# Two-stage layer kernel: the first queries and four key tiles of the attention are fetched and split inside the projection

## What is computed

```
xn  = layernorm(x)
q, k, v = split(xn @ Wqkv + bqkv)            # each 4096 x 512
att = softmax(q @ k.T / sqrt(512)) @ v       # per sequence
z   = xn @ A_w.T                             # 64 experts x rank 8 = 512
z   = z * gate(xn)                           # top 16 of 64 experts, softmax weights
out = x + att @ Wo + bo + 2 * (z @ B_w.T)
```

## Time and profile before

| what | value |
|---|---|
| median of three runs | 2958.62 us |
| the profiled execution, its own time | 2959.48 us |
| its span, first to last instruction | 2957.6 us |
| mean granted TensorE clock | 0.983 |
| TensorE matmul busy | 2772.5 us (94%) |
| VectorE busy | 1858.8 us (63%) |
| ScalarE busy | 931.8 us (32%) |
| GpSimd busy | 736.4 us (25%) |
| DMA, mean over the span | 161 GB/s |

### The profile page before, as it was taken

The page is one execution under the profiler, slowest core; times in us unless marked ns, Lnnn a source line. Parts: engine busy times, 40 slices in busy tenths (PEclk is TensorE's granted clock), DMA queues, the critical chain, the costliest instruction groups (busy, mean ns, idle before and its releaser), DMA issues.

```text
span 2957.6 us, 34124 instructions
## 1 busy us (share of the span) xinstructions
PE 2772.5 (94%) x12096; PEld 2249.8 (76%) x12096; DVE 1858.8 (63%) x2133; ACT 931.8 (32%) x1164; POOL 736.4 (25%) x429
## 2 busy tenths in 40 slices
PE   2888999999999999999889999999999999999999
PEld 1666787878778787888668788787887878878787
DVE  5876777666776777364466655666556665566653
ACT  1222232323232223322244333343433434334331
POOL 7165212030120203020030502305033050330521
PEclk8999999999999999999999999999999999999999
DMA  9767455544554454333533534535445353453544
GB/s 371 232 234 237 153 192 166 183 138 152 187 180 142 163 177 137 115 99 107 180 105 121 174 131 137 178 121 174 130 136 177 122 176 128 136 176 124 175 143 136
DMA packets 261611, 476.34 MB, mean 161 GB/s; under 512 B 26864, under 2 KB 76016, under 8 KB 257264
## 3 DMA queue, kind: packets, MB, share of 16 engines
q1 hardware_dynamic: 223408, 372.45, 39.0%
q10 hardware_dynamic: 29376, 68.72, 6.6%
q0 software_dynamic: 8704, 33.56, 3.2%
HBM read 390.74 MB, written 83.91 MB: 160 GB/s over the span
## 4 chain that ended last, share of the span: by engine, by line
PE 74%; DVE 11%; DMA 4%; issue 4%; ACT 3%; SPq 2%; POOL 2%; DVEq 0%; ACTq 0%; POOLq 0%
PE psum L689 31%; PE psum L1448 13%; PE psum L1450 13%; PE psum L1449 13%; DVE prob L1645 3%; DVE w_lo L739 2%; PE psum L626 2%; DVE r_lo L1617 1%; ACT r_hi L1338 1%; SPq L362 1%; DVE s_lo L744 1%; DVE part L726 1%; DMA t_scratch<-xb 1%; DMA w_raw<-t_scratch 1%; DMA xb<-W_blocks 1%
## 5 line engine op out<-in xcount | busy, mean ns | idle before, releaser
L739 DVE TENSOR_TENSOR w_lo<-w_raw,w_hi 128x1024 fp32r<-128x1024 f32 x224 | 325.7, 1454 | 417.0 <-ACT w_hi L442 416.6
L442 ACT ACTIVATE w_hi<-w_raw 128x1024 fp32r<-128x1024 f32 x224 | 237.4, 1060 | 946.4 <-PE psum L689 812.7
L1617 DVE TENSOR_TENSOR r_lo<-r_raw,r_hi 128x1024 fp32r<-128x1024 f32 x256 | 380.3, 1500 | 189.4 <-ACT r_hi L1338 189.4
L1448 PE MATMUL psum<-r_hi,f_hi 128*128 128x512 f32 x1024 | 405.7, 396 | 30.4 <-DVE r_lo L1617 29.0
L1449 PE MATMUL psum<-r_lo,f_hi 128*128 128x512 f32 x1024 | 400.8, 391 | 0.0
L1450 PE MATMUL psum<-r_hi,f_lo 128*128 128x512 f32 x1024 | 400.6, 391 | 0.0
L689 PE MATMUL psum<-s_hi,w_hi 128*128 128x512 f32 x896 | 356.3, 398 | 40.8 <-DVE w_lo L739 27.6
L1583 POOL TENSOR_TENSOR res<-res,b_out 128x512 f32<-128x512 f32 x128 | 222.8, 1769 | 661.4 <-DMA res<-x 661.4
L689 PE MATMUL psum<-w_hi,s_hi 128*128 128x512 f32 x896 | 353.8, 395 | 32.5 <-DVE w_lo L739 32.4
L689 PE MATMUL psum<-s_lo,w_hi 128*128 128x512 f32 x896 | 352.9, 394 | 0.0
L689 PE MATMUL psum<-s_hi,w_lo 128*128 128x512 f32 x896 | 352.5, 393 | 0.0
(11 more groups left out here) (133 smaller groups left out, 4287.0 us busy)
## 6 DMA issues: line engine op xcount, KB each, us to landing
w_raw<-t_scratch SPq DMA_DIRECT2D x128, 512.0 KB, 3.9
w_raw<-W_blocks SPq DMA_DIRECT2D x96, 512.0 KB, 3.9
r_raw<-k_scratch SPq DMA_DIRECT2D x64, 512.0 KB, 3.8
r_raw<-v_scratch SPq DMA_DIRECT2D x64, 512.0 KB, 4.6
r_raw<-B_T SPq DMA_DIRECT2D x64, 512.0 KB, 3.9
res<-x SPq DMA_DIRECT2D x128, 256.0 KB, 4.9
r_raw<-Wo SPq DMA_DIRECT2D x64, 512.0 KB, 4.5
out<-res SPq DMA_DIRECT2D x128, 256.0 KB, 3.4
```

The source lines that it names most:

```text
L442: nc.scalar.activation(w_hi[:, s % RAW], w_raw[:, s % RAW], ACT.Copy).then_inc(s_whi, 1)
L739: nc.vector.tensor_tensor(w_lo[:, s % RAW], w_raw[:, s % RAW], w_hi[:, s % RAW].bitcast(F32), ALU.subtract).then_inc(s_wlo, 1)
L1448: pe.matmul(bank, sh, mh, start=first, stop=False)
L1617: nc.vector.tensor_tensor(r_lo[:, slot, :], r_raw[:, slot, :], r_hi[:, slot, :].bitcast(F32), ALU.subtract).then_inc(b_lo, 1)
```

## The change

SyncE, at step (5, 1) of the last group (the sixth of seven products), issues the fetch of the first queries and of key items 0 to 3, after waits for what must be free or stored. ScalarE and VectorE, in the steps of the last product, split them: at s = 1 and 2 the two halves of the queries, at s = 4 to 7 the four key items. The corresponding instructions at the start of phase B fall away. The tiles of phase B are declared in another order, so that each early tile lies over a block that is free by then: `r_lo` over `xb` 0, `q_raw` and `q_hi` over block 1, `r_raw` over block 2, `r_hi` over block 3, `q_lo` over `mean_rstd`. `early_stored` waits for the key and query stores of the groups before the last.

```diff
@@ phase_a, sync @@
                             store_kq(g, C22, b)
                             store_kq(g, C12, b)
+                    if not more and (idx, s) == (5, 1):
+                        ahead.sync(sp)
@@ phase_a, scalar (behind split_weights, split_x) @@
+                    if not more and idx == NI - 1:
+                        ahead.scalar(act, s)
@@ phase_a, vector (behind split_weights, take_last_side) @@
+                    if not more and idx == NI - 1:
+                        ahead.vector(dve, s)
@@ phase_a @@
     def early_stored(engine):
-        for c in (C11, C21):
-            engine.wait_ge(s_stK[c], 16 * HT * NG)
-        for c in (C22, C12):
+        for c in range(4):
             engine.wait_ge(s_stK[c], 16 * HT * (NG - 1))
...
+    first.queries_free = lambda engine: engine.wait_ge(s_slo, pair(NG - 1, 2, PART - 1) + 1)
+    first.queries_low_free = lambda engine: engine.wait_ge(s_xn[3], NG * PART)
+    first.raw_free = lambda engine: (engine.wait_ge(s_slo, pair(NG - 1, 3, PART - 1) + 1),
+                                     engine.wait_ge(s_s2, NG * PART))
+    first.high_free = lambda engine: (engine.wait_ge(s_slo, pair(NG - 1, 5, PART - 1) + 1),
+                                      engine.wait_ge(s_s1, NG * PART))
@@ phase_b @@
-    r_raw = sb("r_raw", [P, RING, 2 * W])
+    r_lo = sb("r_lo", [P, RING, 2 * W], F32R)
     q_raw = sb("q_raw", [P, DT, QG])
     q_hi = sb("q_hi", [P, DT, QG], F32R)
+    r_raw = sb("r_raw", [P, RING, 2 * W])
+    r_hi = sb("r_hi", [P, RING, 2 * W], F32R)
     q_lo = sb("q_lo", [P, DT, QG], F32R)
-    r_hi = sb("r_hi", [P, RING, 2 * W], F32R)
-    r_lo = sb("r_lo", [P, RING, 2 * W], F32R)
@@ phase_b, sync @@
-                fetch(t, i, k_scr.rearrange("(m p) t -> p m t", p=P)[:, :, bass.ds(base + i * 2 * P, 2 * P)])
+                if not (static(t) and t == 0 and i < RING):
+                    fetch_keys(t, i, base)
...
-        first.x_used(sp)
-        first.early_stored(sp)
-        queries(0)
+        if early:
+            first.early_stored(sp)
+            first.queries_free(sp)
+            queries(0)
+            first.raw_free(sp)
+            for i in range(RING):
+                fetch_keys(0, i, 0)
+            return
@@ phase_b, scalar @@
-        first.x_used(act)
-        split_queries(0, 0)
-        split_queries(0, 1)
+        if step is not None:
+            if step == 0:
+                first.queries_free(act)
+            if step in (1, 2):
+                split_queries(0, step - 1)
+            if step == 3:
+                first.high_free(act)
+            if step >= IPI - RING:
+                split(0, step - IPI + RING)
+            return
@@ phase_b, vector: the same, with queries_low_free at step 0 and x_used at step 3 @@
@@ phase_b, scores of scalar and vector @@
-            split(t, 0)
+            start = static(t) and t == 0
+            if not start:
+                split(t, 0)
             for i in range(S_IT):
-                if i + 1 < S_IT:
+                if i + 1 < S_IT and not (start and i + 1 < RING):
                     split(t, i + 1)
```

More of the change, by code:

```diff
@@ L93, in layer_kernel @@
         }
+        ahead = Programs()
         with ExitStack() as a_memory:
             first = phase_a(nc, a_memory, whole, psum, common, x, xT, W_blocks, b_cols, WqT, keysT,
-                            k_scr, q_scr, z_scr, v_scr, stat_scr, t_scr, T, C, D, NE, RD, RANK, KT, TG, NG)
-        second = phase_b(nc, whole, psum, common, first, x, Wo, bo, B_T, k_scr, q_scr, z_scr, v_scr, out,
+                            k_scr, q_scr, z_scr, v_scr, stat_scr, t_scr, ahead, T, C, D, NE, RD, RANK, KT, TG, NG)
+        second = phase_b(nc, whole, psum, common, first, ahead, x, Wo, bo, B_T, k_scr, q_scr, z_scr, v_scr, out,
                          T, C, D, S, QG, NQ, KEYT, DT)
@@ L145, in phase_a @@
 def phase_a(nc, memory, whole, psum, common, x, xT, W_blocks, b_cols, WqT, keysT,
-            k_scr, q_scr, z_scr, v_scr, stat_scr, t_scr, T, C, D, NE, RD, RANK, KT, TG, NG):
+            k_scr, q_scr, z_scr, v_scr, stat_scr, t_scr, ahead, T, C, D, NE, RD, RANK, KT, TG, NG):
     NTOK = TG // P
@@ L1117, in phase_a, with phase_b @@
     return first
-def phase_b(nc, whole, psum, common, first, x, Wo, bo, B_T, k_scr, q_scr, z_scr, v_scr, out,
+def phase_b(nc, whole, psum, common, first, ahead, x, Wo, bo, B_T, k_scr, q_scr, z_scr, v_scr, out,
             T, C, D, S, QG, NQ, KEYT, DT):
@@ L1139, in phase_b @@
     EXP_STEP = 4
+    IPI = 8
     def sb(name, shape, dt=F32):
@@ L1250, in out_ready, with sync @@
             engine.wait_ge(b_used, number(u + 1, S_IT + c * OPB + OPB - 1) + 1)
-    def sync(sp):
+    def sync(sp, early=False):
         def fetch(t, it, source):
@@ L1280, in load_block, with fetch_keys @@
                              ).then_inc(b_x[slot], 16)
+        def fetch_keys(t, i, base):
+            fetch(t, i, k_scr.rearrange("(m p) t -> p m t", p=P)[:, :, bass.ds(base + i * 2 * P, 2 * P)])
         def scores(t):
@@ L1331, in sync, with scalar @@
             sp.wait_ge(b_st[slot], 16 * NQ * CB * QT // XO)
-    def scalar(act):
+    def scalar(act, step=None):
         def split(t, it):
@@ L1376, in scores @@
         def scores(t):
-            split(t, 0)
+            start = static(t) and t == 0
+            if not start:
+                split(t, 0)
             for i in range(S_IT):
-                if i + 1 < S_IT:
+                if i + 1 < S_IT and not (start and i + 1 < RING):
                     split(t, i + 1)
-                if i == 0 and not (static(t) and t == 0):
+                if i == 0 and not start:
                     finish_values(t - 1)
@@ L1611, in gpsimd, with vector @@
         output(NQ - 1, False)
-    def vector(dve):
+    def vector(dve, step=None):
         def split(t, it):
@@ L1691, in scores @@
         def scores(t):
-            split(t, 0)
+            start = static(t) and t == 0
+            if not start:
+                split(t, 0)
             for i in range(S_IT):
-                if i + 1 < S_IT:
+                if i + 1 < S_IT and not (start and i + 1 < RING):
                     split(t, i + 1)
-                if i == 0 and static(t) and t == 0:
+                if i == 0 and start:
                     first.take_last(dve)
@@ L1747, in values @@
                     split_queries(t + 1, i - 5)
-        split_queries(0, 0)
-        split_queries(0, 1)
+        if step is not None:
+            if step == 0:
+                first.queries_low_free(dve)
+            if step in (1, 2):
+                split_queries(0, step - 1)
+            if step == 3:
+                first.x_used(dve)
+            if step >= IPI - RING:
+                split(0, step - IPI + RING)
+            return
         segments(dve, scores, output, values)
@@ L1753, in vector @@
         take_output(NQ - 1, CB - 1)
+    ahead.sync = lambda sp: sync(sp, True)
+    ahead.scalar, ahead.vector = scalar, vector
     second = Programs()
```

## The result

The change makes the kernel faster. The median of four runs is 2944.09 us (2942.52 to 2945.57) against 2959.61 us for four runs of the kernel before; the ratio is 0.9943, with a 95% interval of 0.9931 to 0.9956. On the 2958.62 us that the prediction started from, the ratio means 2941.8 us, a gain of 16.8 us (13.0 to 20.4). The forecast was 2944.7 us, a gain of 13.9. The interval of this one comparison takes in the forecast gain.

What follows compares the result with a forecast made beforehand. TensorE is busy 2772.5 of 2957.6 us, but a latency chain idles it at the projection-attention boundary. Gap 12.37 plus slow clock 1.53 less zero costs gives 13.90 us: 2958.62 to 2944.7 us, range 2943.4 to 2949.5.

Steps and rivals of the forecast that it cites:

- the path: Projection to attention boundary: TensorE waits on a pure latency chain, query fetch at 1448.31, landing, then splits; 12.37 us lost.
- the costs of zero: Early fetches on SyncE, early splits on ScalarE and VectorE, and key item 4 were each put at 0 us.
- The early fetches: SyncE at (5, 1): five DMAs, weight load (5, 4) lands 1375.9 to 1377.2, needed by 1379.9; cost 0, at most 9.8 us.
- rival 3: Burst on the queue delays weight load (5, 4); at about 200 GB/s 5.2 us lost, gain 8.7; chance 0.06.
- VectorE's step (6, 6): Last product: the weight split for it ends at 1434.26, then key split 0 at 1435.4, wanted 1436.6; room 1.2 us, cost 0.
- Key item 4: Fetched behind the stores: issued 1459.3, split by 1467.6, wanted 1469.3; room 1.7 us, cost 0, upper bound 1.8 us.
- the moved splits: Six on ScalarE in idle time, six on VectorE in the last product: cost 0, VectorE's upper bound 6.8 us.
- Rival 1: Item 4 or a weight tile a little late, giving back 0.5 to 4 us: 2945.2 to 2948.7; chance 0.12.
- Rival 2: TensorE's own issue limits at the boundary: 0 to 12.4 us, middle price 6 us, gain 8, 2950.7; chance 0.05.
- 13.9 us as the most that can be won: Phase boundary: 12.37 us of TensorE gap plus 1.53 us of slow matmuls, taken as the upper limit of the gain.
- the low end: Lower limit of the forecast range, 2943.4 us: only the spread of the runs goes below the 13.9 us gain.
- the clock term: First seven score matmuls take 3.12 us instead of 1.59 because the clock fell during the gap: 1.53 us.

## Why the prediction was right, and where it was not

**Right: the path.** The gap was the landing of the first fetch behind the stores, and it is gone: 0.23 us at the boundary, and with it the slow matmuls: the step from 59.33 to 45.41 us in the pair of profiles is the whole of the two terms that were read there. The runs with the fetch alone and with the queries alone show the cause, not only the place.

**Right: the costs of zero.** The early fetches: I had the load of step (5, 4) landing at 1375.9 to 1377.2 on the old scale; it was taken at 1373.54 in a projection that ends 3.76 us earlier, so at 1377.3, and TensorE never waited. The 4.19 MB thus moved at some 318 GB/s, an estimate with the 2.3 us of the prediction taken off, and rival 3's fall to 200 GB/s didn't come. Two thirds of a burst more, or the hold of some 7.6 us (both profiles put on one scale by the end of the projection, less TensorE's wait), makes TensorE wait, so this room was real and small. One row was misread without harm: the 2.4 us for issuing four key fetches were taken from behind other traffic as if nothing had been in front, and behind the queries they took 3.52 us. VectorE's step (6, 6): the weight split ends at 1431.72 and is wanted at 1443.75 - 10.9 = 1432.9; room 1.2 us, as worked out. Key item 4: issued at 1455.53, split by 1464.11, wanted at 1443.75 + 21.8 = 1465.5; room 1.4 us against 1.7. None of this decided anything, and the moved splits, which I costed so carefully, turned out not to be needed.

**Rival 1** didn't come either: neither item 4 nor a weight tile was late. **Rival 2, TensorE's own issue:** refuted. The row "issue" of the earlier trace rows was the weight load waiting behind the same thing; with the data there, nothing of the 12.6 us stays.

**Wrong: 13.9 us as the most that can be won, and the low end built on it.** The steps were "12.37 + 1.53 = 13.90 us is the most that this change can win", and "13.9 is the most that can be won, so only the spread of the runs goes below it", with 1.3 us allowed for that spread (2944.7 - 2943.4). Both terms of the sum came from one execution, and it was the mildest of the three that I now have:

| profile | distance at the boundary | slow matmuls | projection to transposes | gain to 45.41 |
|---|---|---|---|---|
| before, of the prediction | 12.60 us | 7 | 59.33 us | 13.9 us |
| before, repeated | 12.94 us | 10 and a part | 60.46 us | 15.1 us |
| before, tiles in new order | 12.78 us | 13 and a part | 60.81 us | 15.4 us |
| changed kernel (3 profiles) and 6 variants with all fetches early | 0.23 us | none | 45.41 or 45.42 us | |

Taken apart, the distance gives 12.4 to 12.7 us and the clock the rest: 60.46 - 45.41 - 12.71 = 2.3 us and 60.81 - 45.41 - 12.55 = 2.9 us, where the profile of the prediction had 1.5. The mean gain of the three is 14.8 us, a ratio of 0.9950. The five comparisons of the changed kernel and of the two with only the fetch early were 0.9943, 0.9951, 0.9948, 0.9953 and 0.9949, in the mean 0.9949 (some of them share their runs of the kernel before). So the likeliest size of the effect is some 15 us, 1 us more than forecast: 0.7 us of it in the clock term, which was put at 1.5 and is 2.2 in the mean, and 0.2 in the distance.

That alone doesn't carry the time out of the range: 14.8 us give 2943.8, which lies inside, and the 15.4 of the largest give 2943.2. The other step that failed is the allowance for spread. The first comparison, 16.8 us, has some 2 us on top of the 14.8, where the low end left 1.3 for everything; the high end of the same range had been given 2. With 15.4 us for the gain and 2 us for the comparison the low end would have been 2941.2. The interval of the first comparison, 13.0 to 20.4, takes in 13.9 as well as 15, so it is the distances at the boundary that show 13.9 to be no upper bound, and not that ratio. The projection alone moves by up to 15 us between profiles. That the projection's 3.8 us in the first pair are spread is shown by the repeats; how much of the first ratio's excess each stretch made is not, since only the profiled executions can be split. Why the number of slow matmuls differs between executions of the same code stays open.

Two smaller slips changed nothing. The slow matmuls stand 0.43 us apart, which is 1.9 times the normal distance and not twice. And the high end should have been 2948.7 + 2 = 2950.7 by its own words, not 2949.5.

## What to carry to other kernels

At the seam of two phases, look for the first fetch of the second and ask what its queue does before it: here it stood behind a wait and at least 2 MB of stores. Moving the fetches ahead (the queries and the key items together; the queries alone gave 3.9 of some 15 us at the boundary) was worth the whole gain at both places tried, while moving the arithmetic behind them gained nothing, since the engines were idle by themselves, with 0.5 us to spare. Price an idle stretch of TensorE as the gap plus the slow matmuls behind it, and take the second from several executions. To judge a change of half a per cent, compare a distance between two marks around it, and not the span. Here it repeated to 0.01 us in the changed kernels; in the kernel before, where TensorE stands idle inside it, it moved by 1.5 us, so there too several executions are needed.

## What the runs showed of the hardware

- After the same idle time of 12.2 to 12.6 us, TensorE ran at the lower of its two clock levels (granted clock 0.50 or 0.51 over these matmuls) for 7, some 11 and some 14 matmuls of 128x512 in three executions: 1.5, 2.3 and 2.9 us lost. After 8.5 us of idle time it was 11 matmuls and 2.2 us. With the gap filled by 52 matmuls the clock was 1.00 and none was slow.
- Issuing a DMA can take SyncE much longer when much is in flight. Four fetches of 0.5 MB took 3.52 us behind 1 MB and 7.19 us behind 3.1 MB, and the weight load after those took 4.1 us to issue by itself, instead of 1.2 in the changed kernel and 0.36 in the kernel before. A burst thus holds up the engine that issues it, not only the data behind it.
- VectorE's subtractions of the maximum (128x512) lasted 0.68 us, or some 1.8 us when they began while GpSimd was adding 128x512 tiles: 5 of 16 in two steps each of two kernels, without an exception. No run tests whether the one causes the other.
